# Linear attention: the denominators from a scan of decayed key sums instead of from products with ones

## The reference, cut to what matters

```python
q, k = elu(x @ Wq) + 1, elu(x @ Wk) + 1          # per head, 64 features
v, a = x @ Wv, sigmoid(x @ Wa + ba + 2)          # a: one decay per head and token
def step(carry, inp):
    S, z = carry
    S = at[..., None, None] * S + kt[..., :, None] * vt[..., None, :]
    z = at[..., None] * z + kt
    num = einsum('bhk,bhkv->bhv', qt, S)
    den = einsum('bhk,bhk->bh', qt, z) + 1e-6
    return (S, z), num / den[..., None]
x1 = layernorm(x + out @ Wo)
```

## Time and profile before

| | us |
|---|---|
| three runs, median (lowest to highest) | 1390.17 (1389.93 to 1392.13) |
| the profiled execution | 1394.7 |
| its span, first to last instruction | 1392.8 |
| PE busy | 1255.3 |
| ACT busy | 937.6 |
| DVE busy | 868.1 |
| POOL busy | 715.1 |

### The profile page before, as it was taken

How to read it: one execution, slowest core, us unless ns; L and a number is a source line. 1 busy time by engine, 2 the same in 40 slices (tenths; PEclk the granted TensorE clock), 3 DMA queues, 4 the chain that set the end, 5 groups by cost and what they waited for, 6 DMA issues and landing times. The chain is left out here.

```text
span 1392.8 us, 29331 instructions
## 1 busy us (share of the span) xinstructions
PE 1255.3 (90%) x10053; PEld 1079.5 (78%) x10053; DVE 868.1 (62%) x1579; ACT 937.6 (67%) x2118; POOL 715.1 (51%) x645
## 2 busy tenths in 40 slices
PE   5999999999999999999899999944999999997870
PEld 4788888888888888887677777724788888887870
DVE  4456565665656565565468888845566666665664
ACT  3778777787777778787557777735465556655553
POOL 1244433444443344444467777701477777776653
PEclk9999999999999999999999999965899999999895
DMA  5232222322222232222134434323466666666638
GB/s 175 90 103 85 93 84 65 90 69 85 77 93 77 64 90 68 87 69 84 56 99 111 106 94 115 89 55 110 129 159 159 159 159 159 158 153 148 175 54 249
DMA packets 155787, 151.27 MB, mean 109 GB/s; under 512 B 48882, under 2 KB 124250, under 8 KB 155674
## 3 DMA queue, kind: packets, MB, share of 16 engines
q1 hardware_dynamic: 140698, 129.18, 30.3%
q0 software_dynamic: 14976, 20.62, 8.3%
HBM read 113.45 MB, written 33.84 MB: 106 GB/s over the span
## 5 line engine op out<-in xcount | busy, mean ns | idle before, releaser
L568 DVE SCALAR_TENSOR_TENSOR a_qk<-a_qk_exp,a_qk_relu 128x512 f32<-128x512 f32 x124 | 148.8, 1200 | 179.8 <-ACT a_qk_relu L416 179.8
L1889 POOL DMA_INDIRECT sum_rows<-e_y_out,e_target x78 | 128.0, 1642 | 81.9 <-ACT e_y_out L1943 58.3
L367 POOL TENSOR_TENSOR a_key_sum<-a_probs_old,a_probs_new 128x512 f32<-128x512 f32 x64 | 83.3, 1301 | 153.2 <-DVE a_probs_new L578 153.2
L360 POOL TENSOR_SCALAR_AFFINE_SELECT a_decay_old<-a_decay_old 128x512 f32<-128x512 f32 x64 | 40.6, 635 | 232.2 <-ACT a_decay_new L442 232.2
L676 PE MATMUL a_ps_qk<-a_xT_hi,a_w_hi 128*128 128x256 f32 x496 | 146.8, 296 | 6.8 <-ACT a_qk_relu L416 6.3
L676 PE MATMUL a_ps_qk<-a_xT_lo,a_w_hi 128*128 128x256 f32 x496 | 139.4, 281 | 0.0
L676 PE MATMUL a_ps_qk<-a_xT_hi,a_w_lo 128*128 128x256 f32 x496 | 139.3, 281 | 0.0
L440 ACT ACTIVATE a_decay_old<-a_c_rows,a_c_col 128x256 f32<-128x256 f32 x256 | 127.4, 498 | 17.6 <-DVE a_c_col L560 11.5
L415 ACT ACTIVATE a_qk_exp<-a_ps_qk 128x512 f32<-128x512 f32 x124 | 73.4, 592 | 95.8 <-PE a_ps_qk L676 95.3
L1870 POOL DMA_INDIRECT e_x_in<-x_rows,e_index x78 | 80.4, 1030 | 78.2 <-DVE e_index L2036 55.7
L576 DVE TENSOR_TENSOR a_probs_old<-a_ps_old,a_decay_old 128x512 f32<-128x512 f32 x128 | 82.3, 684 | 55.8 <-PE a_ps_o L768 44.3
(11 more groups left out here) (310 smaller groups left out, 4170.8 us busy)
## 6 DMA issues: line engine op xcount, KB each, us to landing
a_c_rows<-a_c_scratch SPq DMA_DIRECT2D x128, 256.0 KB, 3.4
e_gu_raw<-in_L_ffn_gate_w SPq DMA_DIRECT2D x23, 512.0 KB
e_gu_raw<-in_L_ffn_up_w SPq DMA_DIRECT2D x23, 512.0 KB
e_dn_raw<-in_L_ffn_down_w SPq DMA_DIRECT2D x23, 512.0 KB, 5.3
a_x_in<-in_x SPq DMA_DIRECT2D x16, 256.0 KB
a_resid<-in_x SPq DMA_DIRECT2D x16, 256.0 KB, 4.8
x_rows<-a_x SPq DMA_DIRECT2D x16, 256.0 KB, 3.4
x_bo_rows<-a_x_bo SPq DMA_DIRECT2D x16, 256.0 KB, 3.9
```

What stands on the lines that cost most here:

```text
L367: pool.tensor_tensor(key_sum[:], probs_old[:, :, P:N], probs_new[:], ALU.add).then_inc(keys_summed, 1)
L568: vec.scalar_tensor_tensor(qk[g][:], qk_exp[buffer][:], 1.0, qk_relu[buffer][:], ALU.min, ALU.add).then_inc(qk_done, 1)
L1889: pool.indirect_dma_start(sum_dram, bass.IndirectOffsetOnAxis(target[par][:, blk:blk + 1], 0), y_out[par][:, blk, :], None, compute_op=ALU ...
```

## The change

The denominators are computed as the reference has them. A second result of ACT, the decay `a` itself (one more exponential of 16x256 per sequence), goes to DRAM and back: SP broadcasts each head's row to 64 partitions (four DMAs of 64 KB per batch). For each batch DVE scans the keys with it (`z = a * z + k`, two scans of 128x256) and multiplies the result in place by the queries (two multiplications of 128x256). POOL splits each product into a rounded part and a remainder (a copy and a subtraction of 128x256 per pair). PE sums over the 64 features of each head with a 128x128 tile that has two blocks of ones, in two products per pair (`add_keys`). The four products with ones per pair, POOL's `sum_keys` and its tile go. DVE runs `sum_states` ahead of `weigh` in each batch, PE runs `add_keys` for both pairs behind both `weighted_values`, and `weigh` now waits for `weighed` instead of `o_made`.

```diff
 SP
+            def store_a(b):
+                sp.wait_ge(a_made, b + 1)
+                sp.dma_start(a_dram[b], z_sb[:]).then_inc(a_stored, 16)
+
+            def spread_a(b, k):
+                m = b * BATCHES + k
+                if k == 0:
+                    sp.wait_ge(a_stored, 16 * (b + 1))
...
+                if m >= 2:
+                    sp.wait_ge(states_done, 2 * (m - 1))
+                for h in range(2):
+                    for p in range(2):
+                        head = 4 * k + 2 * p + h
+                        sp.dma_start(a_rows[m % 2][h * DH:(h + 1) * DH, p, :],
+                                     a_dram[b, head:head + 1, :].to_broadcast([DH, N])).then_inc(a_loaded[m % 2], 16)
 POOL
-            def sum_keys(b, k):
-                pool.wait_ge(probs_done, 3 * (b * BATCHES + k + 1))
-                pool.tensor_tensor(key_sum[:], probs_old[:, :, P:N], probs_new[:], ALU.add).then_inc(keys_summed, 1)
+            def split_sums(b, g):
+                n = b * PAIRS + g
+                pool.wait_ge(q_states_done, n + 1)
+                if n >= 2:
+                    pool.wait_ge(o_made, n - 1)
+                pool.tensor_copy(sum_hi[g % 2][:], states[g % 2][:]).then_inc(sum_hi_done, 1)
+                pool.wait_ge(sum_hi_done, n + 1)
+                pool.tensor_tensor(sum_lo[g % 2][:], states[g % 2][:], sum_hi[g % 2][:].bitcast(F32), ALU.subtract)\
+                    .then_inc(sums_split, 1)
 ACT, log_decay
+                act.wait_ge(dec_done, b + 1)
+                act.activation(z_sb[:], decT[:], ACT.Exp, scale=-1.0).then_inc(a_made, 1)
 DVE
+            def sum_states(b, k):
+                m = b * BATCHES + k
+                vec.wait_ge(a_loaded[m % 2], 64 * (m // 2 + 1))
+                vec.wait_ge(qk_done, 2 * m + 2)
+                for p in range(2):
+                    if m:
+                        vec.wait_ge(sums_split, 2 * m - 1 + p)
+                    vec.tensor_tensor_scan(states[p][:], a_rows[m % 2][:, p, :], qk[2 * k + p][:, 1, :], 0.0,
+                                           ALU.mult, ALU.add).then_inc(states_done, 1)
+                for p in range(2):
+                    vec.wait_ge(states_done, 2 * m + 1 + p)
+                    vec.tensor_tensor(states[p][:], states[p][:], qk[2 * k + p][:, 0, :], ALU.mult).then_inc(q_states_done, 1)
             def weigh(b, k):
-                vec.wait_ge(o_made, 2 * m)
+                vec.wait_ge(weighed, 2 * m)
             def sequence(b, par):
                 for k in range(BATCHES):
+                    sum_states(b, k)
                     weigh(b, k)
 PE, weighted_values
-                for h in range(2):
-                    pe.matmul(out[h][:, 1, 0:P], ones[:], probs_old[:, 2 * h + p, 0:P], start=True, stop=True)
-                pe.wait_ge(keys_summed, m + 1)
-                for h in range(2):
-                    mm = pe.matmul(out[h][:, 1, P:N], ones[:], key_sum[:, 2 * h + p, :], start=True, stop=True)
-                mm.then_inc(o_made, 1)
+                mm.then_inc(weighed, 1)
+
+            def add_keys(b, g):
+                pe.wait_ge(sums_split, b * PAIRS + g + 1)
+                pe.matmul(ps_o[g % 2][:, 1, :], head_ones[:], sum_hi[g % 2][:], start=True, stop=False,
+                          skip_group_check=True)
+                pe.matmul(ps_o[g % 2][:, 1, :], head_ones[:], sum_lo[g % 2][:], start=False, stop=True,
+                          skip_group_check=True).then_inc(o_made, 1)
             def sequence(b, par):
                 for k in range(BATCHES):
                     score(b, k)
                     for pair in pairs_back(b, k, 1):
                         weighted_values(*pair)
+                    for pair in pairs_back(b, k, 1):
+                        add_keys(*pair)
```

More of the change, by code:

```diff
@@ L167, in sem @@
             return sh.semaphore(nc, name)
-        w_raw = [sb(f"a_w_raw{n}", [P, KC, PW]) for n in range(2)]
+        with nc.sbuf_tensor("a_w_raw0", [P, KC, PW], F32) as first_raw:
+            pass
+        states = [sb(f"a_states{n}", [P, N]) for n in range(2)]
+        sum_hi, sum_lo = ([sb(f"a_sum_{x}{n}", [P, N], F32R) for n in range(2)] for x in ("hi", "lo"))
+        a_rows = [sb("a_a_rows0", [P, 2, N])]
+        w_raw = [first_raw, sb("a_w_raw1", [P, KC, PW])]
         w_hi = [sb(f"a_w_hi{n}", [P, KC, PW], F32R) for n in range(3)]
@@ L178, in linear_attention @@
         ident = cross.ident
-        ones, scan_ones = sb("a_ones", [P, DH]), sb("a_scan_ones", [H, N])
+        head_ones, scan_ones = sb("a_head_ones", [P, P], F32R), sb("a_scan_ones", [H, N])
         x_in, resid = sb("a_x_in", [P, NB, D]), sb("a_resid", [P, NB, D])
@@ L194, in linear_attention @@
         probs_old, probs_new = sb("a_probs_old", [P, 4, N]), sb("a_probs_new", [P, 4, P])
-        key_sum = sb("a_key_sum", [P, 4, P])
+        a_rows.append(sb("a_a_rows1", [P, 2, N]))
+        a_dram = nc.dram_tensor("a_a_scratch", [B, H, N], F32).ap()
         rden = [sb(f"a_rden{n}", [P, N]) for n in range(2)]
@@ L228, in linear_attention @@
         decay_exp, decay_masked, probs_done = sem("a_decay_exp"), sem("a_decay_masked"), sem("a_probs_done")
-        keys_summed, o_made, ln_done, rden_done = (
-            sem("a_keys_summed"), sem("a_o_made"), sem("a_ln_done"), sem("a_rden_done"))
+        a_made, a_stored = sem("a_a_made"), sem("a_a_stored")
+        a_loaded = [sem(f"a_a_loaded{n}") for n in range(2)]
+        states_done, q_states_done = sem("a_states_done"), sem("a_q_states_done")
+        sum_hi_done, sums_split, weighed = sem("a_sum_hi_done"), sem("a_sums_split"), sem("a_weighed")
+        o_made, ln_done, rden_done = sem("a_o_made"), sem("a_ln_done"), sem("a_rden_done")
         oT_done, oT_hi_done, oT_lo_done, y_added = (
@@ L308, in spread_c @@
                     .then_inc(rows_loaded[n % ROWS_AHEAD], 16)
+            def store_a(b):
[5 more added lines that the diff above has]
+                    sp.wait_ge(a_stored, 16 * (b + 1))
+                if m == 0:
+                    sp.wait_ge(w_lo_done, 3)
+                if m >= 2:
[5 more added lines that the diff above has]
+                                     a_dram[b, head:head + 1, :].to_broadcast([DH, N])).then_inc(a_loaded[m % 2], 16)
             def sequence(b):
@@ L315, in sequence @@
                         store_c(b + 1)
+                        store_a(b + 1)
                     if ahead < B * PAIRS:
                         spread_c(ahead // PAIRS, ahead % PAIRS)
+                    for batch in range(b * BATCHES + g // 2 + 2, min(b * BATCHES + g // 2 + 3, B * BATCHES)):
+                        if g % 2 == 1:
+                            spread_a(batch // BATCHES, batch % BATCHES)
                     if g == 0 and b + 2 < B:
@@ L332, in _ @@
             store_c(0)
+            store_a(0)
             for g in range(ROWS_AHEAD):
                 spread_c(0, g)
+                if g % 2 == 1:
+                    spread_a(0, g // 2)
             for b in range(B):
@@ L345, in _ @@
                                pattern=[[-1, P]], channel_multiplier=1).then_inc(ident_ready, 1)
-            pool.memset(ones[:], 1.0).then_inc(consts_step, 1)
+            pool.memset(head_ones[:].bitcast(F32), 0.0).then_inc(consts_step, 1)
+            pool.wait_ge(consts_step, 2)
+            for h in range(2):
+                rows = slice(h * DH, (h + 1) * DH)
+                pool.memset(head_ones[rows, rows].bitcast(F32), 1.0).then_inc(consts_step, 1)
+                pool.wait_ge(consts_step, 3 + h)
             pool.memset(scan_ones[:], 1.0).then_inc(consts_step, 1)
             pool.memset(eps_col[:], LN_EPS).then_inc(consts_step, 1)
-            pool.wait_ge(consts_step, 4)
+            pool.wait_ge(consts_step, 6)
             pool.memset(den_eps[:], EPS).then_inc(consts_ready, 1)
@@ L375, in sequence @@
                 for k in range(BATCHES):
-                    sum_keys(b, k)
+                    for p in range(2):
+                        split_sums(b, 2 * k + p)
                     for following in next_batch(b, k):
@@ L546, in keep_z @@
                 vec.wait_ge(z_made, b + 1)
+                vec.wait_ge(a_stored, 16 * b)
                 vec.tensor_scalar(z_sb[:], zT_view, ba_shift[:, 0:1], Z_FLOOR, ALU.add, ALU.max).then_inc(z_kept, 1)
@@ L567, in finish_qk @@
                     vec.wait_ge(s_made, 2 * ((b - 1) * BATCHES + g // 2 + 1))
+                    vec.wait_ge(q_states_done, 2 * ((b - 1) * BATCHES + g // 2 + 1))
                 vec.scalar_tensor_tensor(qk[g][:], qk_exp[buffer][:], 1.0, qk_relu[buffer][:], ALU.min, ALU.add).then_inc(qk_done, 1)
+            def sum_states(b, k):
[7 more added lines that the diff above has]
+                                           ALU.mult, ALU.add).then_inc(states_done, 1)
+                for p in range(2):
+                    vec.wait_ge(states_done, 2 * m + 1 + p)
```

(15 more changed lines are left out.)

## The result

| | median of the runs (lowest to highest), us | profiled execution's span |
|---|---|---|
| before | 1391.15 (1389.93 to 1392.67) | 1392.8 |
| after | 1424.01 (1422.33 to 1424.77) | 1420.1 |

The ratio is 1.0222, with a 95% interval of 1.0201 to 1.0243: slower, by 31 us (the two medians stand 33 apart). Forecast were +23 us and 1413, in a range of 1379 to 1427.

What follows compares the result with a forecast made beforehand. PE bounded the kernel at 40.58 us per sequence; a cycle through three engines would sum to 42.25, 1.67 longer. Over 14 sequences that adds 23 us to 1390.2: 1413 us, range 1379 to 1427.

Steps and rivals of the forecast that it cites:

- The cycle: DVE, ACT and PE: scans ahead of `weigh` delay `exp_decay` and value copies; period 42.25 us against 40.58; chance 0.52.
- 1. D in batch 1 to PE's second value product: Batch 1: from `exp_decay`'s start through the copy of the values to PE's second value product, 2.02 us.
- 2. to the exponential in batch 3: PE works through from that product to batch 3's exponential: 18.30 us less two batches' saving of 0.40, so 17.50.
- 3. to D in batch 3: Batch 3: from that exponential through `finish_qk`, `normalise` and `keep_c` to `exp_decay`, 2.64 us.
- 4. D to E there, then W, then D: Batch 3's `exp_decay` to the `exp_qk` exponential 3.86 us, to `weigh` 4.5, to batch 0's `exp_decay` 1.93.
- 5. D to E in batch 0, W, D: Batch 0's `exp_decay` to the `exp_qk` exponential 3.37 us, then 6.43 through `weigh` to batch 1's `exp_decay`.
- The rival without turns: Scans behind `finish_qk` don't contend with POOL: exponential to `weigh` 3.9 us, not 4.5; 1391 to 1392 us; chance 0.20.
- The rival of a dearer scan: 128 partitions or interleaving with POOL add 0.3 us to each of four scans on the cycle: 1430 us; chance 0.09.
- the turn at `finish_qk`: Rival: `finish_qk` falls past both POOL subtractions, saving 0.35 us twice more; period 40.0, 1382 us; chance 0.13.
- The saving: PE: two rounded products per pair replace four with ones, saving 0.40 us per batch, 1.6 per sequence.
- Outside the fourteen sequences: First and last sequences have half the pattern and more slack; their added time was taken as nothing.
- The rival that PE stays the bound: PE still sets the period, at 38.6 to 39.0 us per sequence: 1362 to 1368 us; chance 0.06.

Runs made afterwards that it cites:

- narrowing `low_oT`: Changed kernel with POOL's `low_oT` subtracting only 16 of 256 columns, other remainders zero: 1393.9 us, ratio 1.0021 to the kernel before, period 40.68 us.
- `keep_c` out of the way in both: In batch 3, `keep_c` directly behind `weigh`: kernel before, 1384.6 us; changed kernel with `sum_states` also moved behind both, 1370.2 us.
- `weigh` and `keep_c` first: Changed kernel with DVE's `sum_states` moved behind `weigh` and, in batch 3, behind `keep_c` too: 1370.2 us, ratio 0.9852 to the kernel before.

## Why the prediction was right

The cycle was the right one; its growth was under-sized. The measured 1424 lies in the range, but 2 us above the band of 1403 to 1422 in which nearly all of this case was put. The steps can be set beside the trace after, in the prediction's order. As there, E is the start of the exponential that feeds `finish_qk`, W that of `weigh` and D that of `exp_decay`.

| step | predicted | after |
|---|---|---|
| 1. D in batch 1 to PE's second value product (438.39 to 440.41) | 2.02 | 2.02 |
| 2. to the exponential in batch 3 (458.35) | 17.50 | 17.94 |
| 3. to D in batch 3 (460.84) | 2.64 | 2.49 |
| 4. D to E there, then W, then D (460.84, 464.70, 471.13) | 3.86 + 6.43 | 3.86 + 6.43 |
| 5. D to E in batch 0, W, D (428.58 to 438.39) | 9.80 | 9.81 |
| sum | 42.25 | 42.55 |

- *The port.* E to W was to be 4.5 if the scans take turns with POOL, 3.9 if they don't. It is 426.59 - 422.15 = 4.44. W to D is 1.99 where 1.93 was forecast, so that their sum is met to 0.01 is partly luck. The rival without turns falls, and narrowing `low_oT` takes 1.8 us off the period as two such stretches would. The turn goes as forecast to POOL's second subtraction, which had waited since 423.70, and not to the scan that stood next in DVE's list. The rival of a dearer scan falls with the median of 670 ns, and the turn at `finish_qk` didn't fall away (1.03 at 423.26).
- *The cycle and its two batches.* That the place ahead of `weigh` is what costs is shown by the move behind it; that it counts in two batches of four by the kernel without scans, whose period is 2.3 us shorter for 2 x 1.2 us.
- *PE.* The saving was over-sized, and this is the term of the sum that was mis-sized. With `keep_c` out of the way in both, the new denominators shorten the period from 40.00 to 38.94, by 1.1 us and not 1.6. In the kernel with `weigh` and `keep_c` first the batches shorten by 0.13, 0.41, 0.31 and 0.20 us. In batch 3 the small turn of `c` (L778) lies between the rounded products and the projection, so PE changes its kind of product once more, which I hadn't counted. Before the turn there is a distance of 0.20 instead of 0.12, and behind it a first distance of 0.23 instead of 0.12:

```profile
422.60 0.28 PE L834 MATMUL a_ps_o<-a_sum_lo,a_head_ones 128*128 128x256 f32 x1
422.80 0.29 PE L778 MATMUL a_ps_mix<-ident,a_cT 16*128 16x16 f32 x2
423.02 0.39 PE L740 MATMUL a_ps_qk<-a_xT_hi,a_w_hi 128*128 128x256 f32 x1
423.25 0.29 PE L740 MATMUL a_ps_qk<-a_xT_lo,a_w_hi 128*128 128x256 f32 x1
```

  In batch 0 the projection starts 0.29 behind the last product with ones, and its second product 0.19 behind that. It starts 0.14 behind the end of ACT's relu (392.66), as where the view lists such a wait, so PE still waits there for `ps_qk`, though not long enough for the view by stretches to show it:

```profile
392.07 0.59 ACT L462 ACTIVATE a_qk_relu<-a_ps_qk 128x512 f32<-128x512 f32 x1
```

```profile
392.51 0.28 PE L834 MATMUL a_ps_o<-a_sum_lo,a_head_ones 128*128 128x256 f32 x1
392.80 0.36 PE L740 MATMUL a_ps_qk<-a_xT_hi,a_w_hi 128*128 128x256 f32 x1
392.99 0.28 PE L740 MATMUL a_ps_qk<-a_xT_lo,a_w_hi 128*128 128x256 f32 x1
```

  For the 0.1 us of batch 2 the cause stays open. Of step 2's 0.44 in the changed kernel, 0.11 is that the first value product behind the wait is followed after 0.34 us instead of 0.23. The rest lies in batch 2 and, for the most part, in batch 3.
- *Outside the fourteen sequences.* I left them at nothing. The fourteen grew by 14 x 1.88 = 26 us in the profiled executions. The last sequence costs 3 more. Its first batch grows by 2.3, and in its later batches the multiplications meet POOL's masks, which are ahead of `weigh` as well, and both stretch. How the 3 us divide among these no run shows:

```profile
699.28 1.13 POOL L400 TENSOR_SCALAR_AFFINE_SELECT a_decay_old<-a_decay_old 128x512 f32<-128x512 f32 x1 [1.36 <-ACT a_decay_new L490]
```

```profile
699.90 1.56 DVE L631 TENSOR_TENSOR a_states<-a_states,a_qk 128x256 f32<-128x256 f32 x2
```

  The stages behind the linear attention take 2 us less, for which I have no cause. Over the nine profiled executions they vary from 705.7 to 711.8 us, though no edit touches them. That makes 27 between the two profiled spans. The runs' medians stand 33 apart, because the profiled execution before lay 3.5 above its median and that after 1.7 below. So of the 11 us by which the forecast missed, 3 are the period and 3 the last sequence. The others are the later stages (2 the other way), the profiled executions against the medians (5), and the median before, 1 above the 1390.2 from which the forecast started.
- *The rival that PE stays the bound* fell by the order of DVE's list alone: with `weigh` and `keep_c` first it is what happens, at 1370.

## What to carry to other kernels

When work moves off the bounding engine to one that is idle 40% of the time, look where in the receiving engine's list it lands: ahead of an instruction that others wait for, it can close a cycle through several engines that is longer than the bound, and its price is then paid there, while behind that instruction it was free here, but for the last sequence. Add up such a cycle from distances of starts, with the copies and waits that only just fit before; here the sum was right within 0.3 of 42.5 us, and the growth of 1.9 within 0.2. VectorE's instructions with both inputs in SBUF are to be counted with the rest of the instruction that GpSimd runs beside them, and with its next one if that has waited longer (the first scan of a batch took 1.22 instead of 0.67 us).

## What the runs showed of the hardware

- A scan over 128 partitions (L627) takes as long as one over 16 (L554 before): 670 ns against 672 in the median, both for 256 elements.
- Scan, multiplication and scalar_tensor_tensor with both inputs in SBUF all wait for POOL and POOL for them. A scan goes from 0.67 to 1.22 us, two multiplications from 0.73 to 1.29 (in the kernel without scans) and to 1.56 beside the masks, the scalar_tensor_tensor from 0.70 to 1.03, POOL's subtraction from 0.73 to 1.18 and its mask of 512 columns from 0.64 to 1.13. With one input in PSUM nothing changes: L639 takes 0.67 to 0.69 in all its 128 executions. A copy with rounding of 128x256 on POOL takes 0.40 and a subtraction 0.73.
